# Attention with relative position terms: a second, position-ordered copy of the input, a patch-by-patch copy-out of one term, and bias rows padded to full depth

## What is computed

```python
t = ln(x) @ W_prep + b_prep                 # 64 channels -> 5 kinds x 8 heads x 32
# 32 windows b of 8 x 8 positions; kinds q_n, q, k, k_m, v
score  = bias
score += einsum('bhod,ohid->bohi', q_n, pat_n)   # term "a": table of relative positions
score += einsum('bhod,bhid->bohi', q, k)
score += einsum('bhid,ohid->bohi', k_m, pat_m)   # term "c": the second term, another table
score  = (score - mean) / std                    # over the 64 positions i
out    = einsum('bohi,bhid->bohd', score, v) @ W_fin + b_fin
# first mixture, per expert e: acc += gate[e] * (gelu(xf @ W1[e] + b1[e]) @ W2[e] + b2[e])
```

## Time and profile before

| | |
|---|---|
| median of 3 runs | 609.45 us (608.86 to 611.24) |
| profiled execution: span | 608.7 us (the page states no other time for it) |
| instructions | 14940 |
| PE busy | 426.7 us, 70% of the span |
| DVE busy | 414.5 us, 68% |
| ACT busy | 300.9 us, 49% |
| POOL busy | 180.3 us, 30% |
| units of the first half, first a unit to first score | 32.90 to 103.85 us |

### The profile page before, as it was taken

The page is one execution under the profiler, slowest core; times in us unless marked ns, Lnnn a source line. Parts: engine busy times, 40 slices in busy tenths (PEclk is TensorE's granted clock), DMA queues, the critical chain, the costliest instruction groups (busy, mean ns, idle before and its releaser), DMA issues.

```text
span 608.7 us, 14940 instructions
## 1 busy us (share of the span) xinstructions
PE 426.7 (70%) x5883; PEld 316.4 (52%) x5883; DVE 414.5 (68%) x709; ACT 300.9 (49%) x521; POOL 180.3 (30%) x120
## 2 busy tenths in 40 slices
PE   0589997986999978336666534574326998899870
PEld 0367786734777864133333223573215777677650
DVE  7865387787637868666778877415792886787760
ACT  4823587235238822336866645423601765576550
POOL 7000000011000000222323476003004588788872
PEclk9965555987555579767867765599555998899995
DMA  4000000000000084430322000033100122222222
GB/s 139 1 2 2 2 1 1 3 1 1 1 2 1 2 323 162 176 121 27 104 78 79 27 1 1 2 118 152 69 0 27 22 34 33 30 32 33 32 23 39
DMA packets 14359, 28.96 MB, mean 48 GB/s; under 512 B 8328, under 2 KB 8970, under 8 KB 12876
## 3 DMA queue, kind: packets, MB, share of 16 engines
q1 hardware_dynamic: 7292, 23.71, 11.1%
q0 software_dynamic: 7008, 4.36, 5.5%
HBM read 25.21 MB, written 4.03 MB: 48 GB/s over the span
## 4 chain that ended last, share of the span: by engine, by line
PE 46%; DVE 26%; DMA 9%; issue 8%; ACT 6%; POOL 3%; DVEq 0%; ACTq 0%; POOLq 0%
PE ps L454 7%; PE ps L464 7%; PE ps L721 5%; DMA arena<-rows_x,arena 4%; DMA out<-arena 3%; DVE arena L1156 3%; PE ps L441 3%; DVE arena L1256 3%; DVE arena L1233 2%; PE ps L434 2%; PE ps L499 2%; PE ps L443 2%; DVE mu L1056 2%; PE ps L632 2%; DVE arena L1072 2%
## 5 line engine op out<-in xcount | busy, mean ns | idle before, releaser
L721 PE MATMUL ps<-arena 128*128 128x128 f16 x936 | 76.9, 231 | 4.7 <-DVE arena L1380 1.4
L985 POOL TENSOR_TENSOR arena<-arena 128x512 f16<-128x512 f32 x8 | 9.3, 1157 | 233.1 <-ACT arena L846 233.1
L935 ACT ACTIVATE arena<-ps 128x384 f32<-128x384 f32 x78 | 38.2, 490 | 72.4 <-PE ps L721 72.1
L721 PEld LDWEIGHTS ps<-arena 128*128 x936 | 57.3, 102 | 17.9 <-issue 11.7
L1380 DVE TENSOR_TENSOR arena<-ps,arena 128x384 f32<-128x384 f32 x78 | 43.5, 558 | 27.5 <-ACT arena L935 23.6
L1127 DVE TENSOR_TENSOR arena<-ps,arena 128x512 f16<-128x512 f32 x16 | 42.0, 2625 | 20.7 <-ACT arena L817 20.2
L1018 POOL DMA_INDIRECT arena<-rows_x,arena x39 | 40.6, 1040 | 50.2 <-DVE arena L1346 38.6
L404 PE MATMUL ps<-ident,arena 128*128 128x128 f16 x128 | 14.8, 305 | 57.8 <-DVE arena L1072 55.6
L454 PEld LDWEIGHTS ps<-arena 128*128 128x128 f16 x768 | 45.4, 124 | 10.6 <-DVE arena L1119 5.5
L454 PE MATMUL ps<-arena 128*128 128x32 f16 x768 | 46.8, 234 | 4.2 <-DVE arena L1119 4.2
L464 PEld LDWEIGHTS ps<-arena 128*128 128x128 f16 x768 | 45.3, 124 | 5.3 <-issue 3.9
(11 more groups left out here) (204 smaller groups left out, 1120.2 us busy)
## 6 DMA issues: line engine op xcount, KB each, us to landing
arena<-in_wc SPq DMA_DIRECT2D x8, 1024.0 KB, 10.4
arena<-in_w SPq DMA_DIRECT2D x16, 384.0 KB, 3.1
arena<-in_w SPq DMA_DIRECT2D x1, 1536.0 KB, 6.3
arena<-in_numbers SPq DMA_DIRECT2D x1, 1024.0 KB, 8.6
rows_x<-arena SPq DMA_DIRECT2D x1, 1024.0 KB, 3.9
arena<-in_wprep SPq DMA_DIRECT2D x1, 640.0 KB, 4.5
arena<-rows_x,arena POOLq DMA_INDIRECT x39, 2.6
sum_odd<-in_zeros SPq DMA_DIRECT2D x1, 544.0 KB, 8.5
```

The source lines that it names most:

```text
L721: mm = pe.matmul(bank(2 * w + half)[:, c * P:(c + 1) * P], wt.rearrange("p a n -> p (a n)"), xb[b % 2][:, i * P:(i + 1) * P], start=(i == ...
```

## The change

`XH` and `XL`, which the attention did not use before, take a second copy of the input, ordered by position with the 32 windows of a position side by side (`by_position`); it is made ahead of the window-ordered copies. All eight banks take the transposes of the attention, so these no longer wait for a copy-out. n and m move `XH`/`XL`, and the a and c matmuls then move 32 neighbouring elements. The c copy-out reads PSUM with a step of 32 f32 and writes runs of 8. The bias rows become 128 rows deep (2 used, the others zero, set by GpSimd), the tile of ones is 128 x 128, and a v unit takes one bias matmul of 512 columns instead of four of 128. One transfer (`ones`) goes.

```diff
+        def by_position(copy, g, s):
+            src = bank(2 * g + s).bitcast(F16)[:, 0:BANK].rearrange("p (j b v) -> p j v b", j=4, v=8)
+            dst = (XH, XL)[s].rearrange("p (u v h b) -> p u v h b", u=8, v=8, h=2)
+            u0 = 4 * (g % 2)
+            return copy(dst[:, u0:u0 + 4, :, g // 2, :], src)
...
-            src = bank(2 * (g % 2) + s).bitcast(F16)[:, 0:BANK]
+            src = bank((2 * g if L == 0 else 2 * (g % 2)) + s).bitcast(F16)[:, 0:BANK]
...
         def cols_c(CX, k):
-            v = CX.rearrange("p b (u y v) -> p u y v b", u=8, y=2)
-            return v[:, 2 * (k % 4):2 * (k % 4) + 2, k // 4, :, :]
+            v = CX.rearrange("p b (u y v) -> p b u y v", u=8, y=2)
+            return v[:, :, 2 * (k % 4):2 * (k % 4) + 2, k // 4, :]
+        def by_window(o):
+            return o.rearrange("p (u v b) -> p b u v", u=2, b=NW)
...
-                    if g >= 2:
+                    if L and g >= 2:
                         pe.wait_ge(xs_hi, NG * L + g - 1)
                         pe.wait_ge(xs_lo, NG * L + g - 1)
...
                 pe.wait_ge(wp_rdy, 1)
-                pe.wait_ge(xs_hi, NG)
-                pe.wait_ge(xs_lo, NG)
+                pe.wait_ge(xo_hi, NG)
+                pe.wait_ge(xo_lo, NG)
...
+                    if N < 8:
+                        pe.wait_ge(xs_hi, N // 2 + 1)
+                        pe.wait_ge(xs_lo, N // 2 + 1)
...
+                    if kind in "nm":
+                        col = TYPE[kind] * 256 + hg * P
+                        for i, xs in enumerate((XH, XL)):
+                            mm = pe.matmul(o, WP[:, col:col + P], XW(xs, k), start=(i == 0), stop=(i == 1))
+                    elif kind in "qk":
...
                     elif kind == "v":
+                        pe.matmul(o.rearrange("p (b n) -> p b n", b=4), onesP[:],
+                                  bv2[:, hg * P:(hg + 1) * P].unsqueeze(1).broadcast_to([P, 4, P]), start=True, stop=False)
                         for b4 in range(4):
                             b = 4 * k + b4
                             ob = o[:, b4 * P:(b4 + 1) * P]
                             for i, xs in enumerate((XHw, XLw)):
-                                pe.matmul(ob, xs[:, b * P:(b + 1) * P],
-                                          WP[:, 1024 + hg * P:1024 + (hg + 1) * P], start=(i == 0), stop=False)
-                            mm = pe.matmul(ob, ones2[:], bv2[:, hg * P:(hg + 1) * P], start=False, stop=True)
+                                mm = pe.matmul(ob, xs[:, b * P:(b + 1) * P],
+                                               WP[:, 1024 + hg * P:1024 + (hg + 1) * P], start=False,
+                                               stop=(b4 == 3 and i == 1))
...
-                                               mv[:, 8 * oi + oj::PW], start=(i == 0), stop=(i == 2))
+                                               mv[:, (8 * oi + oj) * NW:(8 * oi + oj + 1) * NW], start=(i == 0), stop=(i == 2))
...
-                                               mv[:, 8 * ii + ij::PW], start=(i == 0), stop=(i == 2))
+                                               mv[:, (8 * ii + ij) * NW:(8 * ii + ij + 1) * NW], start=(i == 0), stop=(i == 2))
...
-                            pe.matmul(o, ones2[:], b2r[:], start=True, stop=False)
+                            pe.matmul(o, onesP[:], b2r[:], start=True, stop=False)
...
+                if L == 0:
+                    for g in range(NG):
+                        act.wait_ge(ln_tp, g + 1)
+                        by_position(act.copy, g, 0).then_inc(xo_hi, 1)
...
-                    ins = act.copy(cols_c(Ch, k), o.rearrange("p (u v b) -> p u v b", u=2, b=NW))
+                    ins = act.copy(cols_c(Ch, k), by_window(o))
...
+            pool.memset(onesP[:], 1.0).then_inc(pad_rdy, 1)
+            pool.memset(bv2[:], 0.0).then_inc(pad_rdy, 1)
+            pool.memset(b2r[:], 0.0).then_inc(pad_rdy, 1)
             pool.wait_ge(zeroed, 2)
+            pool.wait_ge(pad_rdy, 3)
...
+                if L == 0:
+                    for g in range(NG):
+                        dve.wait_ge(ln_tp, g + 1)
+                        by_position(dve.tensor_copy, g, 1).then_inc(xo_lo, 1)
...
-                            ins = dve.tensor_tensor(cols_c(Cl, k), o.rearrange("p (u v b) -> p u v b", u=2, b=NW),
-                                                    cols_c(Ch, k), ALU.subtract)
+                            ins = dve.tensor_tensor(cols_c(Cl, k), by_window(o), cols_c(Ch, k), ALU.subtract)
```

More of the change, by code:

```diff
@@ L182, in build @@
         bv2f, bv2h = at(130 * K, 256)[0:2, :], at(125 * K + 512, 256, F16)[0:2, :]
-        b2r = sb("b2r", [2, 512], F16)
+        b2r = sb("b2r", [P, 512], F16)
         small = sb("small", [P, 64])
@@ L192, in build @@
         m1, m2, sm = [sb(n, [P, NT]) for n in ("m1", "m2", "sm")]
-        bv2 = sb("bv2", [2, 256], F16)
-        ones2 = sb("ones2", [2, P], F16)
+        bv2 = sb("bv2", [P, 256], F16)
+        onesP = sb("onesP", [P, P], F16)
         mu = sb("mu", [P, NT])
@@ L218, in build @@
         en1_hi, en_rdy, em_rdy, v_free = [sem(s) for s in ("en1_hi", "en_rdy", "em_rdy", "v_free")]
-        LD_SMALL = 14 * 16
+        xo_hi, xo_lo, pad_rdy = sem("xo_hi"), sem("xo_lo"), sem("bias_rows_padded")
+        LD_SMALL = 13 * 16
         XD = {1: 2, 2: 2 + 16, 3: 2 + 16 + 2}
@@ L343, in _ @@
                              (wff.rearrange("p g c -> p (g c)"), "wfin"), (sel[:], "sel"), (bv2f, "bv"),
-                             (ones2[:], "ones"), (small[:], "small"), (identf[:], "identf"), (FW[:], "dft")):
+                             (small[:], "small"), (identf[:], "identf"), (FW[:], "dft")):
                 sp.dma_start(dst, inp[src]).then_inc(ld_small, 16)
@@ L401, in norm_transposes @@
                     for s in range(2):
-                        dst = bank(2 * (g % 2) + s).bitcast(F16)
+                        dst = bank((2 * g if L == 0 else 2 * (g % 2)) + s).bitcast(F16)
                         for j in range(4):
@@ L428, in unit @@
                             pe.wait_ge(unit_free, count("nmqkac", hg, n - 8))
-                    if kind in "nmqk":
+                    if kind in "nm":
[3 more added lines that the diff above has]
+                    elif kind in "qk":
                         col = TYPE[kind] * 256 + hg * P
@@ L1090, in _ @@
             dve.wait_ge(bv_hi, 1)
-            dve.scalar_tensor_tensor(bv2[:], bv2h, mask[0:2, 9:10], bv2f, ALU.mult, ALU.add)
+            dve.wait_ge(pad_rdy, 3)
+            dve.scalar_tensor_tensor(bv2[0:2, :], bv2h, mask[0:2, 9:10], bv2f, ALU.mult, ALU.add)
             dve.wait_ge(wf_hi, 1)
@@ L1244, in ffn0 @@
                 dve.wait_ge(f0_hi, 1)
-                dve.scalar_tensor_tensor(b2r[:], b2H, mask[0:2, 9:10], b2f, ALU.mult, ALU.add).then_inc(f0_rdy, 1)
+                dve.scalar_tensor_tensor(b2r[0:2, :], b2H, mask[0:2, 9:10], b2f, ALU.mult, ALU.add).then_inc(f0_rdy, 1)
                 norm(1)
```

## The result

The changed kernel takes 538.89 us (median of 4 runs, 536.47 to 540.17), beside 609.15 for the kernel before in the same runs: a ratio of 0.8838, 95% interval 0.8807 to 0.8868. The forecast was 544, range 530 to 568. The profiled execution took 540.17 us, of which 538.1 are its span.

The account below looks back on a forecast made before the run. The prediction took TensorE's attention units, two stretches totalling 142 of 608.7 us, as the bound. Halves -66.3, start +3.3, first mixture -1.3 and scores -1.0 sum to -65.3: 543.4, forecast 544 us, range 530 to 568.

Parts of the forecast that it names:

- What bounded the kernel, and the moving side: Attention units: TensorE bound; table matmuls moving elements 128 bytes apart fall from 57 to 27.5 ns, a unit to 1.32 us.
- The rival that the step was not the cost: Table matmuls: the moving side's step is not what costs, only v and the tail gain; 595 us, chance 0.03.
- The v unit: Attention's v matmuls: 2.05 to 1.28 us, 0.77 us going each time the array changes between 2 and 128 rows.
- The c copy-out: ScalarE and VectorE copies of c from PSUM: 1.04 us each, from 2.51 and 2.63; bounds 0.6 and 2.6.
- The first rival: c copy-out: strided PSUM reads cost what the strided writes did, copies stay at 2.6 us; 574 us, chance 0.12.
- A half: Each half of the attention units: 36.5 us plus 1.3 of tail, 37.8 us; 33.1 saved, 66.3 for two.
- everything at its lower bounds: Rival for the whole kernel: copies at 0.6 to 0.7 us, warm clock, start at its lower bounds; 532 us, chance 0.15.
- The tail before: End of a half in the old kernel: 3 us, the last c unit's two copies behind the last v.
- The second bound: Units at 2.4 GHz: TensorE 28.6 us a half; the clock rises at times but helps little, VectorE's 33 to 36 take over.
- The start: Before the first a unit: four more ScalarE copies at 0.8 us each and GpSimd memsets (+0.5); +3.3 us.
- The rest: Stages outside the units: first mixture's bias matmuls -1.3 us, scores of both halves -1.0 us.
- The warm clock that was hoped for at the scores: First 80 score matmuls of a half: a warm clock saves up to 1.9 us a half, 1 us counted for both.

Follow-up runs that it names:

- k_parts: The changed kernel with the table cast moved ahead on ScalarE and VectorE following ScalarE's k units part by part: 530.15 us, ratio 0.8614.
- c_copy_alone: The kernel before with only the new c copy-out added: 611.42 us, ratio 0.9925.
- changed_again: The changed kernel unaltered, run again beside other versions on the same chip: 542.24 us, ratio 0.8803.

## Why the prediction was right, and where it was off

*What bounded the kernel, and the moving side*: right. The pitch was read as 27.5 ns and is 27 to 28 at the lower clock, 25 at the full one; the reasoning from the gate's 8-column matmuls and the scores was confirmed by undoing the step (61.9 us a half; the sum says 61 and a tail). The rival that the step was not the cost is out.

*The v unit*: right alone (1.25 us at the lower clock for 1.28), and -12.1 us for the 16 x 0.77 = 12.3 of its expectation. The prediction's "0.77 us go each time the array changes" is the sum of four shallow matmuls, some 0.2 us each. In the first mixture it reckoned 0.2 us each, measured 0.23.

*The c copy-out*: mis-sized. The step "I take 1.04 for both engines, the nearest row by step" failed; the copies take 0.59 and 0.68, at the lower bound of 0.6. L1140, from which 1.04 came, reads its stepped operand in SBUF; a stepped read of PSUM costs nothing here. The first rival, for which the rule of the Trainium skill spoke (PSUM — Partial Sum Buffer, Specifications), is refuted for copies by ScalarE and VectorE; what it says of matmuls no run here shows.

*A half*: "I take 36.5 us" plus 1.3 against 34.0 measured, which is 3.8 us too much, twice. VectorE's own sum of 36 was too high by the c copies (8 x 0.36 = 2.9) and by tables reckoned at 0.50, which follow each other every 0.41 us (0.7). The other 2 us to its 30.3 busy us are of the same kind: one instruction starts before the last has ended, and of the m units 2.5 us were left and not 3.1:

```profile
32.92 4.68 DVE L1155 SCALAR_TENSOR_TENSOR arena<-ps,bprep,arena 128x512 f16<-128x512 f32 x7
...
43.25 1.29 DVE L1149 TENSOR_TENSOR arena<-ps,biasT 128x512 f32<-128x512 f32 x2
```

Two L1149 of 0.68 us take 1.29 together. And the clock came up for good rather than at times, 0.94 in the window. The waits for ScalarE's k parts, 3.4 us a half, were not in the sum, only in its last paragraph; k_parts shows that they lay on the path. So two errors partly cancelled: the work was 5.7 us too high, the waits 3.4 too low. In the halves it is the rival "everything at its lower bounds" (0.15) that came true, with 37.8 - 3.5 = 34.3 us; the start, the scores and the stages behind did not follow it, and so the time, 538.9, lies between its 532 and the forecast's 544.

*The tail before*: "3 us" is 70.95 - 8 x 8.5; with the 8.54 of the same rows it is 2.6, and c_copy_alone took 2.1 of it.

*The second bound*: TensorE's total at the full clock was given as 28.6 us; its busy time is 29.2. Right. But "it helps little: VectorE takes over" was too plain: three runs each added work to one engine, and each time part of it showed.

*The start*: +3.3 forecast, +2.2 measured. The position-ordered copies cost 0.58 on ScalarE, not 0.8; of four, 2.3 us. GpSimd's memsets are 0.23, 0.31 and 0.52 us, as reckoned. L1087 again ended with GpSimd's work twice. Up to the first transpose this profile gained 0.36 us (18.28 for 18.64) rather than losing 0.5, and that is luck: the first transpose starts at 18.3 us in four of the other profiles and at 18.6 to 18.8 in nine, and c_copy_alone, without the new memsets, is one of the four. Where it starts later, as in changed_again, the first a unit comes at 35.56 us, and the start costs 2.7 us.

*The rest*: the stages between, -0.7 us beside -1.3, and the step from scores to the second half -1.0, as much as was counted for both together. The warm clock that was hoped for at the scores did not last: in the first half they began at 1.00 (69.08 us), behind 3.2 us in which TensorE was idle, but the clock was 0.74 in their first microsecond, 0.50 from 70 to 72 and 1.00 from 73 on; in the second half they began at 0.50 (145.08) and reached 1.00 at 148. In the kernel before it took from 103.85 to 109.4 us.

All in all, signs and mechanism were right and the gain was 5 us larger than forecast. Against the sum's 543.4 the two halves are 7.6 us shorter and the start 1.1, the other stages 0.6 longer and the last stage 2.8: 543.4 - 7.6 - 1.1 + 0.6 + 2.8 = 538.1, the measured span.

## What to carry to other kernels

Before calling small matmuls slow for their size, count the blocks of 16 bytes in which the moving elements lie: at 2 ns each they set the pitch here, 60 ns at either clock, and with steps of 128 bytes the clock stayed at 0.50 through the units. Where a copy-out must turn something around, let it read PSUM with the step and write in runs: that cost nothing here, the reverse four times the copy. And price an edit by the path that is left after the others: the copy-out was worth 4.6 us without the other edits and 24 with them. When one engine follows another over parts of a tile, let it follow part by part. And before moving work off one engine, look whether the next one has a gap left.

## What had not been expected of the hardware

Beside the free stepped read of PSUM:

- Steps that leave two elements in a block of 16 bytes (33 ns, beside 25 at the same clock) are not free, and steps of 128 bytes (57 ns, in the kernel before) are no dearer than steps of 16 (60 ns).
- Writing f16 at a step of 256 bytes costs 2.44 to 2.63 us for 512 elements on both engines, where the same copy in runs takes 0.59 and 0.68.
- A matmul of 2 rows among matmuls of 128 rows costs some 0.2 us beyond its columns (0.83 / 4 at 2.4 GHz, 0.80 / 4 at 1.2 GHz, 0.23 in the first mixture), nearly the same at either clock.
- TensorE can be busy without a gap for 50 us at a granted clock of 0.50, when its moving elements lie 128 bytes apart.
